# Dropout, matmul and layer norm on one core: the loads of the 8192 x 8192 matrix split between SyncE's and ScalarE's DMA queues

## What is computed

```
keep   = (u >= 0.1)
x_drop = x * keep / 0.9
y      = x + adj @ x_drop
out    = (y - mean(y)) / sqrt(var(y) + 1e-5)     # over the 64 columns
```

## Time and profile before

| | us |
|---|---|
| median of three runs | 657.78 |
| the profiled execution | 659.25 |
| its span, first to last instruction | 657.5 |
| TensorE matmuls busy | 492.7 (75%) |
| VectorE busy | 42.7 (6%) |
| ScalarE busy | 6.0 (1%) |
| DMA queue q1, share of the 16 engines | 96.5% |
| HBM traffic | 272.63 MB read, 2.10 MB written |

### The profile page before, as it was taken

How to read it: one execution, slowest core, us unless ns; L and a number is a source line. 1 busy time by engine, 2 the same in 40 slices (tenths; PEclk the granted TensorE clock), 3 DMA queues, 4 the chain that set the end, 5 groups by cost and what they waited for, 6 DMA issues and landing times.

```text
span 657.5 us, 4821 instructions
## 1 busy us (share of the span) xinstructions
PE 492.7 (75%) x2112; PEld 156.1 (24%) x2112; DVE 42.7 (6%) x210; ACT 6.0 (1%) x9; POOL 13.9 (2%) x15
## 2 busy tenths in 40 slices
PE   0587787786887697686796687877787688868784
PEld 0122222221222222222232222322232122312221
DVE  3000002000020001100020000200002000110002
ACT  0000000000000000000000000000000000000000
POOL 0000001000000000000000000000000000000000
PEclk9997989998989998998999988998999988999888
DMA  9999999999999999999999999999999999999980
GB/s 375 425 442 419 443 426 434 431 435 429 437 429 429 437 425 441 431 425 437 435 427 431 439 425 437 427 433 437 429 435 427 436 431 437 425 431 436 429 358 16
DMA packets 11094, 274.81 MB, mean 418 GB/s; under 512 B 1232, under 2 KB 1232, under 8 KB 2512
## 3 DMA queue, kind: packets, MB, share of 16 engines
q1 hardware_dynamic: 9936, 272.63, 96.5%
q10 hardware_dynamic: 1152, 2.10, 0.8%
HBM read 272.63 MB, written 2.10 MB: 418 GB/s over the span
## 4 chain that ended last, share of the span: by engine, by line
DMA 68%; PE 18%; issue 12%; DVE 1%; another core or an unknown queue 1%; SPq 0%; POOLq 0%; POOL 0%; ACT 0%; DVEq 0%
DMA raw<-adj_dram 68%; PE acc L109 17%; POOLq L35 0%; DVE normed L187 0%; POOL rstd L201 0%; PE turned L117 0%; DVE stats L174 0%; SPq L89 0%; SPq L94 0%; DVE rows L170 0%; DVE moments L178 0%; ACT sums L144 0%; SPq L87 0%; SPq L86 0%
## 5 line engine op out<-in xcount | busy, mean ns | idle before, releaser
L109 PE MATMUL acc<-raw,dropped 128*64 128x512 f32 x2048 | 483.6, 628 | 150.4 <-DMA raw<-adj_dram 150.4
L109 PEld LDWEIGHTS acc<-raw,dropped 128*64 128x64 f32 x2048 | 148.4, 144 | 479.7 <-issue 279.7
L170 DVE TENSOR_TENSOR rows<-turned,x_sb 128x512 f32<-128x512 f32 x8 | 5.5, 692 | 586.3 <-PE turned L117 586.3
L201 POOL TENSOR_TENSOR rstd<-var_eps,minus_half 128x8 f32<-128x8 f32 x8 | 13.1, 1640 | 638.5 <-DVE var_eps L181 638.5
L187 DVE TENSOR_SCALAR normed<-rows,moments,rstd 128x64 f32<-128x64 f32 x64 | 15.0, 310 | 14.1 <-POOL rstd L201 14.1
L117 PE MATMUL turned<-eye,sums 128*128 128x128 f32 x64 | 9.3, 288 | 5.5 <-ACT sums L144 5.5
L117 PEld LDWEIGHTS turned<-eye,sums 128*128 128x128 f32 x64 | 7.7, 191 | 12.5 <-ACT sums L144 12.5
L144 ACT COPY sums<-acc 128x512 f32<-128x512 f32 x8 | 4.7, 586 | 640.6 <-PE acc L109 640.6
L174 DVE BATCH_NORM_STATS2 stats<-rows 128x6 f32<-128x64 f32 x64 | 8.9, 212 | 0.3
L178 DVE BATCH_NORM_AGGREGATE moments<-stats 128x2 f32<-128x6 f32 x64 | 5.1, 153 | 0.3
L163 DVE TENSOR_TENSOR dropped<-dropped,x_sb 128x4096 f32<-128x4096 f32 x1 | 4.4, 4426 | 2.7 <-DMA x_sb<-x_dram 2.7
## 6 DMA issues: line engine op xcount, KB each, us to landing
raw<-adj_dram SPq DMA_DIRECT2D x63, 4096.0 KB, 31.5
dropped<-u_dram SPq DMA_DIRECT2D x1, 2048.0 KB, 7.7
x_sb<-x_dram SPq DMA_DIRECT2D x1, 2048.0 KB, 12.2
out_dram<-normed ACTq DMA_DIRECT2D x8, 256.0 KB, 14.3
raw<-adj_dram SPq DMA_DIRECT2D x1, 2048.0 KB, 26.9
raw<-adj_dram SPq DMA_DIRECT2D x1, 1024.0 KB, 29.0
raw<-adj_dram SPq DMA_DIRECT2D x2, 512.0 KB, 30.1
```

Of the source, the lines that this page charges most:

```text
L109: last = nc.tensor.matmul(acc[t * D:(t + 1) * D, :], dropped[:, c, :], raw[:, i % SLOTS, j, t * BANK:(t + 1) * BANK], start=(c == 0), stop ...
L170: nc.vector.tensor_tensor(rows[:, :, :], turned[:, :, :], x_sb[:, b * GROUP:(b + 1) * GROUP, :], ALU.add).then_inc(rows_ready, 1)
L201: nc.gpsimd.tensor_tensor(rstd[:, :], var_eps[:, :], minus_half[:, :], ALU.pow).then_inc(rstd_ready, 1)
```

## The change

SyncE issues u, the pieces of slots 0 and 2, and nothing else. ScalarE issues x, the pieces of slots 1 and 3, and the four parts of piece 63, between its other work. In ScalarE's program, the loads of rounds 2b + 1 and 2b + 2 stand ahead of `take_sums(b)` and `store(b)`. The last load ahead of `take_sums(b)` waits for the last piece of block b, which `take_sums(b)` waits for as well. Slots, sizes, conditions of the waits, and the work of TensorE, VectorE and GpSimd are as before.

```diff
--- before.py
+++ after.py
@@ -81,24 +81,18 @@
 
         block = ctx.enter_context(nc.Block())
 
+        rounds = BLOCKS * ROUNDS
+
         @block.sync
         def _(sp):
+
             sp.dma_start(dropped[:, :, :], u_dram).then_inc(u_loaded, DMA)
-            sp.dma_start(x_sb[:, :, :], x_dram).then_inc(x_loaded, DMA)
-            for s in range(SLOTS):
+            for s in (0, 2):
                 sp.dma_start(raw[:, s, :, :], adj[s]).then_inc(raw_loaded[s], DMA)
-            rounds = BLOCKS * ROUNDS
-            with sp.Fori(1, rounds - 1) as g:
-                for s in range(SLOTS):
+            with sp.Fori(1, rounds) as g:
+                for s in (0, 2):
                     sp.wait_ge(multiplied, (g - 1) * SLOTS + s + 1)
                     sp.dma_start(raw[:, s, :, :], adj[g * SLOTS + s]).then_inc(raw_loaded[s], DMA)
-            for s in range(SLOTS - 1):
-                sp.wait_ge(multiplied, (rounds - 2) * SLOTS + s + 1)
-                sp.dma_start(raw[:, s, :, :], adj[(rounds - 1) * SLOTS + s]).then_inc(raw_loaded[s], DMA)
-            sp.wait_ge(multiplied, LAST - SLOTS + 1)
-            for f, (c0, c1) in enumerate(FINE):
-                sp.dma_start(raw[:, SLOTS - 1, c0:c1, :],
-                             adj[LAST][:, c0 * BLOCK:c1 * BLOCK]).then_inc(fine_loaded[f], DMA)
 
         @block.tensor
         def _(pe):
@@ -148,7 +142,28 @@
                 act.dma_start(out_dram[:, b * GROUP * D:(b + 1) * GROUP * D],
                               normed[:, :, :]).then_inc(out_stored, DMA)
 
+            def load(g, s):
+                act.wait_ge(multiplied, (g - 1) * SLOTS + s + 1)
+                act.dma_start(raw[:, s, :, :], adj[g * SLOTS + s]).then_inc(raw_loaded[s], DMA)
+
+            def load_fine():
+                act.wait_ge(multiplied, LAST - SLOTS + 1)
+                for f, (c0, c1) in enumerate(FINE):
+                    act.dma_start(raw[:, SLOTS - 1, c0:c1, :],
+                                  adj[LAST][:, c0 * BLOCK:c1 * BLOCK]).then_inc(fine_loaded[f], DMA)
+
+
+            act.dma_start(x_sb[:, :, :], x_dram).then_inc(x_loaded, DMA)
+            for s in (1, 3):
+                act.dma_start(raw[:, s, :, :], adj[s]).then_inc(raw_loaded[s], DMA)
             for b in range(BLOCKS):
+
+                for g in range(b * ROUNDS + 1, min((b + 1) * ROUNDS + 1, rounds)):
+                    load(g, 1)
+                    if g < rounds - 1:
+                        load(g, 3)
+                    else:
+                        load_fine()
                 take_sums(b)
                 store(b)
             act.wait_ge(out_stored, BLOCKS * DMA)
```

## The result

The changed kernel takes **666.3 us** (median; 665.88 to 666.74) against 657.75 for the kernel before on the same chip: ratio 1.0125, 95% interval 1.0107 to 1.0142. The profiled execution took 666.74, its span is 665.0, against 659.25 and 657.5 before.

A forecast was written before the change was run, and what follows sets the result against it. Bound: arrival of the last bytes plus what the engines still owe then. Issuing, start and rate 0 each, order of arrival with cold clock +7.9 on a median of 657.78: 665.7 us, range 659 to 671.

The forecast's parts named there:

- Issuing: Loads issued by SyncE and ScalarE: SyncE had time and ScalarE is nearly idle, so gain 0 and cost 0.
- start: First pieces: 0 and 1 land together at about 32.8, TensorE starts 10 us later; cost 0, bound under 1.3 us.
- rate: Mid-stream loads: same bytes at the same rate, taken as 0; bounds 3.2 us of loss, some 3 us of gain.
- Order of arrival: End of the stream: queues alternate by packet, 61 lands last of the whole pieces, TensorE owes three pieces, not two: +7.9 us.
- E: End of the loads: the time when the last part of piece 63 lands, 640.9, claimed to stay.
- Store 6 lets 60 and 62 go ahead: Last loads: store 6 takes turns of ScalarE's queue, so 61 is the last whole piece to land, at 631.05.
- The case of queues in step: End of the stream: 60 and 61 land together while 62 waits; +2.2 to +5.7 us at full clock, up to 2.3 more cold.
- The clock, 2.31: Last three pieces on TensorE: after some 10 us idle the first takes 9.40 instead of 7.09, adding 2.31 us.
- The sum: Whole kernel: 23.58 us owed against 15.65 gives +7.9, other terms 0; median 657.78 + 7.9 = 665.7.
- Rival 1: Load queues: turns of whole DMAs or arrival in order of issue, so nothing changes, 657.8 us; chance 0.07.
- rival 2: Changes between DMAs: the second queue fills gaps, faster, 652.5 us at 0.2 us a piece; chance 0.08.
- rival 3: Block ends in mid-stream: both queues run dry, +4.9 us on top of +7.9, 670.6; chance 0.07.

The follow-up runs named there:

- e1: The changed kernel with its last four pieces (60 to 63) all issued by SyncE: 658.31 us, ratio 0.9999 to the kernel before.
- e3: The changed kernel with each piece of slots 0 and 2 loaded as two DMAs of half rows (16 KB packets): 669.56 us in a single run.
- e9: The changed kernel with ScalarE issuing the store of block 6 behind the load of piece 61 instead of ahead of it: 661.56 us, ratio 1.0058.
- e2: The changed kernel with the eight stores issued by GpSimd instead of ScalarE: 663.02 us, ratio 1.0077.
- e5: The changed kernel with 22 extra matmul calls, all writing one half of the PSUM rows, between piece 60 and the wait for 61: 672.69 us.
- e7: The changed kernel with 22 extra matmul calls, alternating between PSUM halves, between piece 60 and the wait for 61: 667.47 us, ratio 1.0122.
- e10: The changed kernel with 13 extra matmul calls, alternating between PSUM halves, between piece 60 and the wait for 61: 665.64 us, ratio 1.0118.
- e6: The kernel before (one queue) with piece 62 loaded as two halves with a semaphore each: 655.86 us, ratio 0.9963.

## Why the prediction was right

Forecast 665.7 for the median (range 659 to 671, slower 0.82), measured 666.3. Point by point:

- *Issuing, start, rate: 0 each.* Right by e1: with all but the last round split, the ratio is 0.9999. The 0 of the start has a bound that I didn't name: in e3, where TensorE starts at 42.28 instead of 32.72, both queues run dry. A detail was wrong: x is issued at 0.75 us, ahead of ScalarE's table load and not behind it; the load of the table now comes before the first copy, at 107.86, 1.28 us in the first block, where loads hide it.
- *Order of arrival.* Right, and the step that carries it, one packet from each queue in turn whatever its size, is shown by the even counts beside the stores and, for packets of two large sizes, by e3. 61 was forecast at 631.05 and landed at 630.5. E was forecast unchanged at 640.9 and is 640.5.
- *Store 6 lets 60 and 62 go ahead.* Right by e9 and e2, which take it away in two ways and get back 4.7 and 3.3 us.
- *The case of queues in step* (+2.2 to +5.7 at full clock, for the end of the matmuls) is what e2 made: 649.10 against 646.70, +2.4. With 62 landing at 634.9 my formula for it, landing plus 14.2, gives 649.1.
- *The clock, 2.31.* The three pieces took 23.22 - 21.27 = 1.95 more than my three at full clock. That it is the idle time ahead of them that costs it is shown by e5, e7 and e10.
- *The sum.* 23.22 - 15.65 = 7.57, less 0.44 for 61's earlier start, and 0.37 in the finish (turn to end 10.48 us instead of 10.11), give 7.5: the difference of the spans, where I had 7.9. The medians differ by 8.55: the profiled execution before stood 1.5 above its median, that of the changed kernel only 0.44 above its own. The term mis-sized for the median is the 15.65 from which I subtracted: it holds the dip that, as it seems (e6), only some executions of the kernel before have. With 14.18 in its place the forecast would have been 667.2. The cold term, too large by 0.36, and the 0.44 of 61 hid part of it, so that an error of only 0.6 us in the median is in part luck.
- *Rival 1* (no change) would have needed pieces arriving singly; *rival 2* (gaps filled) a higher rate than before, but mid-stream windows have 432 GB/s in both, and E moved by 0.4 us only; *rival 3* (starvation) slices below 9 in mid-stream, of which there is none. I had expected pairs with waits of 4 to 5 us throughout; so it is for the first pairs only, then the wait behind each store grows to 16, by the same slippage that stands at the end.

## What to carry to other kernels

A stream that fills the DMA engines gains nothing from a second queue (0.9999 with sixty of 64 pieces split), and it loses order: two queues deliver in turns of a packet, so that two loads in step both land when only the second would have, and each small packet of a store gives up a turn that the other queue fills with 32 KB. A store of 0.6 us by its bytes made the load behind it land 5.3 us later. At the end of a stream count what the engine still owes when the last bytes land, pieces and clock together; keep the last pieces on one queue in the order of use, and cut them finer, which on one queue won 2.9 us here.

## What the runs showed of the hardware that I had not expected

- With the same loads and full DMA engines, pieces arrived in more than one lasting pattern in mid-stream: one wait of up to 15.8 us a block in the changed kernel, e1, e5 and e9, two waits of 5.5 and 8.2 us a block in e7, of 5.5 and 5.6 in e10. What picks between them stays open.
- Matmuls of 64 columns of weights that all go to one half of the PSUM rows took 18.62 us for some 43 (e5), and 9.61 us for 44 when they alternated between the halves (e7): calls to the two halves overlap, those to one half don't.
- A store from GpSimd's queue lands about as soon as one from ScalarE's own: 15.5 us in e2 against 14.3 before, both beside loads, where behind loads in ScalarE's queue it took 27.8 (medians of eight). GpSimd's stores are fewer packets, 640 for the eight instead of 1152, so they need 5 turns on a DMA engine instead of 9, now beside two queues of loads.
